# A depthwise 3x3 term moved from VectorE, ScalarE and GpSimd to TensorE, in a fused attention and expert block

## The chip, the core and the metric

The kernel runs on one core of one Trainium2 chip. The metric is the device time of one execution in microseconds (us); lower is better. All data are float32.

## What is computed

The input x is (8, 64, 96, 96). The reference, cut to what matters here:

```python
def _window_attend(xh, qkv_w, lepe_w, bias, sp, heads, scale):      # xh: 32 channels
    qkv = jnp.einsum('oi,bihw->bohw', qkv_w, xh)
    q, k, v = jnp.split(qkv, 3, axis=1)
    lepe = jax.lax.conv_general_dilated(v, lepe_w, (1, 1), 'SAME', feature_group_count=c)
    ...                                                              # windows of 4x4 pixels, 8 heads
    out = jnp.einsum('nhqk,nhkc->nhqc', attn, v) + lepe
    ...
for s in (0, 2):                                                     # plain and rolled by 2
    xs = jnp.roll(x, (-s, -s), axis=(1, 2)) if s > 0 else x          # axes 1, 2: channels, rows
    halves = (xs[:, :c], xs[:, c:])
    ...                                                              # attend each half, roll back
x = x + (results[0] + results[1])                                    # of the normalized x
t = tokens of x
t = t + top-2-of-8 experts (64 to 64 channels each) of the normalized t
```

So there are four attention problems per image (two halves of the channels, plain and rolled by two channels and two rows), each with a depthwise 3x3 convolution of its value channels (`lepe`). Their sum is added to x, and a mixture of eight experts follows.

## The kernel before

**Tiling.** An image has 24 strips of four rows (384 pixels); two strips are a tile, 12 per image and 96 in all. A strip has 24 windows, done in three units of eight windows. The program runs through 576 slots, one per unit, so a strip is 3 slots and a tile is 6 slots. Every step has a lag in slots (`LAG`): in each slot every engine does, in the order in which its body lists them, the steps whose turn it is. Lags set how far apart producer and consumer stand; the engines are otherwise held together by semaphores, and each engine works strictly in its written order. The loop body holds 72 slots (one image) and is written out, so that all instructions of an image are distinct; a head of one image and a tail of nearly two stand outside it.

**Stages.** For each tile the input is loaded, centred and normalized over channels (`centre`, `variance`), and stored to a buffer `xn` in DRAM; from there it is loaded again as strips with all four problems on the 128 partitions (`load_strips`). For each strip TensorE makes the values (`value`, L612), and a second time, in another channel order, the values for the convolution (`wo`, L615); then queries and keys (`query_key`, L624 and L625). GpSimd issues the DMAs that spread keys and values (L516, L528). For each unit TensorE computes the scores (L585, 64 small matmuls with 64 loads), VectorE takes the row maximum and subtracts it (L904, L909), ScalarE exponentiates (L742) and lays the bias for a later unit into the score bank (L748), VectorE transposes (L969), and TensorE forms the products with the values (L652) and, in the last unit of a strip, the sums (L658). ScalarE inverts the sums (L714, L716), VectorE multiplies (`divide`, L922, into `att`).

**The convolution before.** ScalarE copies the values of L615 from PSUM into a padded image `vpad` in SBUF (L737). Of the nine taps ScalarE multiplies three (L780), GpSimd adds these three (L547), and VectorE does the other six as multiply-adds, two per slot (L896). VectorE then adds the result to `att` and reorders it into rows (`add_taps`, L955, into `fin`). SyncE stores `fin` to `z` in DRAM (L427).

**The tile stage.** When all strips that a tile needs are in `z`, SyncE loads x, the plain part `z0t` and the rolled part `z2t` (`load_tile`, ten DMAs, L449 and L454). VectorE adds them (L935, L948), then come a second normalization, the router (L682), the logits turned by TensorE (L636), the choice of two experts on VectorE, the gates turned by three TensorE transposes (L594), stored and spread over partitions by eight DMAs per tile (L474, L484), multiplied into the normalized tokens by VectorE (L884), and four pairs of expert matmuls (L570: two halves of 64 output channels, each with 128 input rows), on top of a bias matmul (L689). VectorE adds and SyncE stores the result.

**What sets the order around the change.** The products of a strip's first unit may only start when `divide` of the strip before has read the one bank of products, `bank_o` (`pe.wait_ge(picked, k)`, L646). The bank `bank_p[1]` is shared by the second value matmul, the keys, the variances and the router; `bank_g` holds the turned gates and the logits. SyncE does its DMA issues and waits in one strict order, and `load_tile` waits there for the `z` it has just stored to land (L438).

## Time and profile before

| | us |
|---|---|
| median of 3 runs | 3483.31 |
| lowest and highest run | 3472.05, 3487.7 |
| the profiled execution: its span, first to last instruction | 3495.3 |
| busy in it: TensorE / VectorE / GpSimd / ScalarE | 3038.4 / 3088.6 / 2932.3 / 2038.3 |
| mean granted TensorE clock, as a share of 2.4 GHz | 0.925 |

The profiled execution's own time was not listed apart from its span; the span lies 0.3% above the median of the runs and 0.2% above the highest. PE is TensorE, DVE VectorE, ACT ScalarE, POOL GpSimd, SP SyncE.
### The profile page before, as it was taken

Reading aid. Unit: us, or ns where it says so; the run is one execution under the profiler, and the core shown is the slowest. Engines: PE = TensorE matmul, PEld = TensorE weight load, DVE = VectorE, ACT = ScalarE, POOL = GpSimd, SP = SyncE. Lnnn points to the kernel's source line nnn. Section 1 sums busy time; section 2 is a strip of 40 time slices with the busy share of each in tenths; the row PEclk is TensorE's granted clock in tenths of the full one; section 3 lists DMA queues with packets and bytes.
Section 4 is the critical chain, followed back from the end, with each engine's and each line's share of the span. In section 5 each row is a group of like instructions: output and inputs, shape, how many; then the busy total and the mean of one; then the engine's idle time right before and its main releaser. Section 6 shows DMA issues by size and latency. Waiting matters only on the chain.

```text
span 3495.3 us, 200950 instructions
## 1 busy us (share of the span) xinstructions
PE 3038.4 (87%) x82372; PEld 1892.0 (54%) x82372; DVE 3088.6 (88%) x6049; ACT 2038.3 (58%) x4130; POOL 2932.3 (84%) x5382
## 2 busy tenths in 40 slices
PE   5889888888898888998888988889899899889886
PEld 3655555555555555555555555555555555555551
DVE  3789999889999888998999889999899899999995
ACT  3666666556565556665666656566556656666651
POOL 5998888888898788987888878889788988888970
PEclk8999999999899899998999989999899989999986
DMA  2345555545555455545555544555455555555555
GB/s 58 85 122 147 137 143 138 143 130 143 136 144 139 125 144 137 145 130 133 136 139 140 139 131 130 143 135 143 130 140 138 143 134 145 137 143 137 138 124 151
DMA packets 427432, 469.79 MB, mean 134 GB/s; under 512 B 117616, under 2 KB 407920, under 8 KB 426480
## 3 DMA queue, kind: packets, MB, share of 16 engines
q1 hardware_dynamic: 260592, 342.97, 36.3%
q0 software_dynamic: 165888, 113.57, 13.5%
q8 instruction: 665, 10.90, 1.4%
q14 instruction: 287, 2.35, 0.2%
HBM read 264.97 MB, written 77.86 MB: 98 GB/s over the span
## 4 chain that ended last, share of the span: by engine, by line
PE 36%; DVE 22%; issue 14%; DMA 12%; SPq 9%; POOL 3%; ACT 3%; DVEq 1%; ACTq 0%; POOLq 0%
PE bank L585 9%; PE bank L652 8%; SPq L454 6%; DMA gate_wide<-gate_rows 6%; DVE lepe L896 6%; DMA z<-fin 5%; PE bank L570 5%; DVE row_max L904 3%; PE bank L658 2%; PE bank L612 2%; POOL vx L528 2%; PE bank L624 2%; DVE probT L969 2%; SPq L449 1%; DVE gx L884 1%
## 5 line engine op out<-in xcount | busy, mean ns | idle before, releaser
L528 POOL DMA_DIRECT2D vx<-vt x3072 | 1555.5, 515 | 201.9 <-PE bank L658 181.0
L652 PEld LDWEIGHTS bank<-probT,vx 128*32 128x32 f32 x36864 | 825.8, 188 | 442.4 <-issue 378.2
L652 PE MATMUL bank<-probT,vx 128*32 128x16 f32 x36864 | 888.2, 234 | 170.7 <-issue 117.5
L516 POOL DMA_DIRECT2D kx<-k_sb x1536 | 738.8, 488 | 230.9 <-issue 114.6
L585 PEld LDWEIGHTS bank<-kx,qx 32*32 32x32 f32 x36864 | 602.9, 112 | 434.9 <-issue 432.2
L585 PE MATMUL bank<-kx,qx 32*32 32x64 f32 x36864 | 709.9, 227 | 128.5 <-issue 90.9
L742 ACT ACTIVATE prob<-prob 128x512 f32<-128x512 f32 x576 | 367.4, 638 | 538.9 <-DVE prob L909 538.6
L896 DVE SCALAR_TENSOR_TENSOR lepe<-vpad,table,lepe 128x384 f32<-128x384 f32 x960 | 630.8, 657 | 0.0
L884 DVE TENSOR_TENSOR gx<-gate_wide,yn_pair 128x768 f32<-128x768 f32 x384 | 393.8, 1026 | 194.4 <-DMA gate_wide<-gate_rows 148.0
L547 POOL TENSOR_TENSOR lepe_p<-lepe_p,tap_sb 128x384 f32<-128x384 f32 x384 | 435.0, 1133 | 39.0 <-issue 18.5
L904 DVE TENSOR_REDUCE row_max<-bank 128x32 f32<-128x512 f32 x576 | 394.4, 685 | 29.5 <-PE bank L585 16.4
L909 DVE TENSOR_TENSOR prob<-bank,row_max 128x512 f32<-128x512 f32 x576 | 398.4, 692 | 16.7
L969 DVE STREAM_TRANSPOSE probT<-prob 128x512 f32<-128x512 f32 x576 | 405.3, 704 | 0.0
L570 PE MATMUL bank<-gx,table 128*64 128x384 f32 x1536 | 357.2, 542 | 15.6 <-DVE gx L884 14.4
L748 ACT ACTIVATE bank<-bias_tile 128x512 f32<-128x512 f32 x576 | 341.0, 592 | 0.0
L538 POOL DMA_DIRECT2D yn_pair<-yn x384 | 201.3, 532 | 67.5 <-DVE gx L884 43.0
L756 ACT ACTIVATE qx<-bank,table 128x384 f32<-128x384 f32 x384 | 200.7, 575 | 62.2 <-PE bank L624 62.1
L780 ACT ACTIVATE tap_sb<-vpad,table 128x384 f32<-128x384 f32 x384 | 232.8, 606 | 2.0 <-POOL lepe_p L547 2.0
L625 PE MATMUL bank<-xs,table 32*32 32x384 f32 x1536 | 200.6, 549 | 14.1 <-issue 14.1
L624 PE MATMUL bank<-xs,table 32*32 32x384 f32 x1536 | 200.1, 545 | 5.2 <-issue 3.8
L735 ACT ACTIVATE v_sb<-bank 128x384 f32<-128x384 f32 x192 | 93.2, 485 | 176.6 <-PE bank L612 173.4
L612 PE MATMUL bank<-xs,table 128*128 128x384 f32 x384 | 169.7, 524 | 20.5 <-DMA xs<-xn 20.5
(75 smaller groups left out, 3801.9 us busy)
## 6 DMA issues: line engine op xcount, KB each, us to landing
gate_wide<-gate_rows SPq DMA_DIRECT2D x768, 192.0 KB
vx<-vt POOLq DMA_DIRECT2D x3072, 12.0 KB
kx<-k_sb POOLq DMA_DIRECT2D x1536, 24.0 KB
z<-fin SPq DMA_DIRECT2D x192, 192.0 KB, 4.3
yn_pair<-yn POOLq DMA_DIRECT2D x384, 96.0 KB
xa<-in_x SPq DMA_DIRECT2D x192, 96.0 KB, 3.3
xn<-xa SPq DMA_DIRECT2D x192, 96.0 KB
xs<-xn SPq DMA_DIRECT2D x96, 192.0 KB
```

The source lines that it names most:

```text
L516: pool.dma_start(kx[to + m:to + C:4, r % 2, m, :], k_sb[at + m:at + C:4, r % 2, :])\
L528: pool.dma_start(vx[to:to + TOK, r % 2, col:col + 13:4, odd, :], vt[at:at + TOK, r % 2, x::2, :, :].rearrange("p h n k -> p h (n k)"))\
L547: G.tensor_tensor(lepe_p[:, kr % 2, :], lepe_p[:, kr % 2, :], tap_sb[:, j - 1, :], ALU.add).then_inc(pool_lepe_made, 1)
L570: last = MM(bank_f[half * C:(half + 1) * C, 0:SPX], const("experts")[:, p * C:(p + 1) * C], gx[:, p % 2, half, :], start=False, stop=(p == ...
L585: last = MM(bank_s[r % 2][at, w * KEYS:(w + 1) * KEYS], qx[at, kr % 2, win, :, :].rearrange("p a i -> p (a i)"), kx[at, kr % 2, :, win * T ...
L652: last = MM(bank_o[32 * c:32 * c + 32, at * TOK:(at + 1) * TOK], vx[:, kr % 2, :, at % 2, at // 2 * 4 + ba], probT[:, kr % 2, at, ba * TOK ...
L742: S.activation(prob[:, r % 4, :], prob[:, r % 4, :], ACT.Exp).then_inc(exp_made, 1)
L884: V.tensor_tensor(gx[:, p % 2, :, :], gate_wide[:, p, :, :], yn_pair[:, r % 2, :, :], ALU.mult)\
L896: V.scalar_tensor_tensor(acc, vrows(r, t // 3 - 1, t % 3 - 1), lepe_taps[:, t:t + 1], first if j == 0 else acc, ALU.mult, ALU.add).then_in ...
L904: V.tensor_reduce(row_max[:, r % 2, :], per_row(bank_s[r % 2][:, :]), AX.X, ALU.max).then_inc(max_made, 1)
L909: V.tensor_tensor(per_row(prob[:, r % 4, :]), per_row(bank_s[r % 2][:, :]), over_keys(row_max[:, r % 2, :]), ALU.subtract).then_inc(shifte ...
L969: V.transpose(probT[:, kr % 2, j * UW:(j + 1) * UW, :].rearrange("p n k -> p (n k)"), prob[:, r % 4, :]).then_inc(probT_made, 1)
```

## The change

The convolution acts on the values, which are a linear map of the normalized x. The change joins both: for each output channel, tap and input channel it builds a weight once at the start (VectorE, from tables: tap times value weight, plain and rolled parts added), so that the four depthwise terms become a single 3x3 convolution from 64 to 64 channels of `xn`, done on TensorE per tile of eight rows, where the sum with x is formed.

- SyncE loads, per tile, ten rows of `xn` twice, the second copy one row further (`load_halo`, two DMAs of 64 partitions by 3840 bytes; four at the two tiles at the image's edge). With two rows on the 128 partitions a matmul does two taps of a column.
- TensorE does three groups of matmuls per tile, one for each column offset, in the slots with lags 34, 35 and 36. A group is four matmuls of 128 rows by 64 columns over 384 pixels: two halves of the tile, which go to the two halves of the PSUM partitions, by two weight sets (rows one and two, row three with zeros). At the edge of an image some are cut into pieces.
- The second value matmul, its copy to `vpad`, and all taps on ScalarE, GpSimd and VectorE are gone; `divide` writes `fin` directly, and PE's wait on `picked` becomes one on `fin_made`, counted on the same instruction. VectorE adds three terms instead of two per tile (`y_first` now reads the convolution's bank).
- The convolution takes `bank_g`. The logits and the gates go through `bank_p[1]`; three transposes of gates become one of 48 columns, and the bias matmul of the experts becomes three over 128 pixels.

The diff, cut to its core:

```diff
 LAG = dict(
     ...
-    tap_products=15, pool_taps=16, taps=19, add_taps=24,
-    store_z=24, load_tile=33, y_first=37, y_second=38, ..., router=41, logits=42,
-    take_logits=43, gates=45, ...
+    store_z=24, load_halo=29, load_tile=33, conv=34, y_first=37, y_second=38, y_third=38, ..., router=41, logits=44,
+    take_logits=44, gates=45, ...
 # SyncE
+                if ti := s.tile("load_halo"):
+                    k, r = ti
+                    if s.later(r, 2):
+                        wait_alone(sp, conv_made, k - 1)
...
+                        put_halo(0, 0, t * (2 * SP) - 1, HALO)
+                        put_halo(1, 0, t * (2 * SP), HALO)
 # GpSimd
-                if st := s.in_strip("pool_taps"):
-                    k, kr, j = st
-                    if j:
-                        pool.wait_ge(tap_made, k * POOL_TAPS + (j + 1))
...
-                        G.tensor_tensor(lepe_p[:, kr % 2, :], lepe_p[:, kr % 2, :], tap_sb[:, j - 1, :],
-                                        ALU.add).then_inc(pool_lepe_made, 1)
 # TensorE
             pe.wait_ge(table_loaded, 16)
+            pe.wait_ge(conv_w_made, 1)
...
-                    for blk in range(TBLK):
-                        last = nc.tensor.transpose(bank_g[0:GE, blk * 128:(blk + 1) * 128],
-                                                   gate_tmp[:, 4, blk * GE:(blk + 1) * GE], const("ident"))
-                    last.then_inc(gateT_made, 1)
+                    nc.tensor.transpose(bank_p[1][0:TBLK * GE, 0:128], gate_tmp[:, 4, :], const("ident"))\
+                        .then_inc(gateT_made, 1)
...
                     MM(bank_p[0][:, 0:SPX], wv, xs[:, r % 4, :], start=True, stop=True).then_inc(v_made, 1)
-                    if r % 2:
-                        pe.wait_ge(ln_made, tiles_to(s, (k - 1) // 2 + 3))
-                    MM(bank_p[1][:, 0:SPX], wo, xs[:, r % 4, :], start=True, stop=True).then_inc(vo_made, 1)
...
+                if (ti := s.in_tile("conv")) and ti[2] < len(SIDES):
+                    k, r, side = ti
+                    t, dw = (r + 1) % IMT, SIDES[side]
+                    if side == 0:
+                        pe.wait_ge(halo_loaded[r % 2], halos_to(s, r) * 16)
+                        if s.later(r, 1):
+                            pe.wait_ge(y_step, k * 2 - 1)
+                    low, high = max(0, -dw), W - max(0, dw)
+                    first = [side == 0, side == 0]
+                    for group, skip in ((0, 0), (1, 2)):
+                        parts = [(half, *rows) for half in range(2) for rows in conv_rows(t, half)[group]]
+                        for half, top, end, which in sorted(parts, key=lambda part: part[1]):
+                            at = half * SP + skip
+                            last = MM(by_rows(bank_c[half * C:(half + 1) * C, 0:SPX])[:, top:end, low:high],
+                                      conv_w[:, which, group * 3 + side, :],
+                                      by_rows(halo[:, r % 2, :])[:, at + top:at + end, low + dw:high + dw],
+                                      start=first[half], stop=(side == 2 and group == 1), skip_group_check=True)
+                            first[half] = False
+                    if side == 2:
+                        last.then_inc(conv_made, 1)
...
-                            pe.wait_ge(picked, k)
+                            pe.wait_ge(fin_made, k)
...
-                    MM(bank_f[:, 0:SPX], const("expert_bias", GE), gateT[:, r % 2, :], start=True, stop=True)
+                    for blk in range(TBLK):
+                        MM(bank_f[:, blk * 128:(blk + 1) * 128], const("expert_bias", TBLK * GE)[:, blk * 128:(blk + 1) * 128],
+                           gateT[:, r % 2, :], start=(blk == 0), stop=True, skip_group_check=True)
 # ScalarE
-                    act.wait_ge(vo_made, k + 1)
-                    S.activation(vrows(r, 0, 0), bank_p[1][:, 0:SPX].rearrange("p (r w) -> p r w", w=W),
-                                 ACT.Copy).then_inc(v_saved, 1)
...
-                    S.activation(product.rearrange("p (r w) -> p r w", w=W), vrows(r, -1, j - 1), ACT.Copy,
-                                 scale=lepe_taps[:, j:j + 1]).then_inc(tap_made, 1)
 # VectorE
-            V.memset(vpad[:, :], 0.0).then_inc(const_made, 1)
             dve.wait_ge(table_loaded, 16)
+            ...                               # seven operations of 128 x 384 or 64 x 384 that build conv_w
...
-                    V.tensor_tensor(att[:, r % 2, :], bank_o[:, 0:SPX], row_inv[:, r % 2, :], ALU.mult).then_inc(picked, 1)
+                    V.tensor_tensor(windows(fin[:, r % 2, :]), by_window(bank_o[:, 0:SPX]),
+                                    by_window(row_inv[:, r % 2, :]), ALU.mult).then_inc(fin_made, 1)
...
-                    V.tensor_tensor(y[:, r % 4, :], xt[:, r % 2, :], z0t[:, r % 2, :], ALU.add).then_inc(y_step, 1)
+                    dve.wait_ge(conv_made, k + 1)
+                    V.tensor_tensor(y[:, r % 4, :], bank_c[:, 0:SPX], xt[:, r % 2, :], ALU.add).then_inc(y_step, 1)
...
-                    V.tensor_tensor(windows(fin[:, r % 2, :]), by_window(att[:, r % 2, :]),
-                                    windows(lepe[:, r % 2, :]), ALU.add).then_inc(fin_made, 1)
...
-                taps = s.in_strip("taps")
-                if taps:
-                    tap(taps[0], taps[1], 2 * taps[2])
...                                           # y_second adds z0t, the new y_third adds z2t
-                if taps:
-                    tap(taps[0], taps[1], 2 * taps[2] + 1)
```

## Rows read from the trace of the kernel before

**Rows 1.** The page: busy us of each engine (share of span) and instructions

```profile
PE 3038.4 (87%) x82372; PEld 1892.0 (54%) x82372; DVE 3088.6 (88%) x6049; ACT 2038.3 (58%) x4130; POOL 2932.3 (84%) x5382
```

**Rows 2.** Busy time by stretch: five of 500 us, the last and their sum

```profile
core 0: us, PE busy (x) PEld busy (x) DVE busy (x) ACT busy (x) POOL busy (x), PEclk, DMA share, GB/s
2500.00:3000.00 500.00, 448.51 (x12219) 280.39 (x12219) 454.17 (x898) 303.41 (x616) 434.28 (x800) 0.94 0.53 138
sum 2500.00, PE 2211.04 PEld 1382.66 DVE 2254.99 ACT 1491.45 POOL 2144.69; mean PE 442.21 PEld 276.53 DVE 451.00 ACT 298.29 POOL 428.94
```

**Rows 3.** Timeline, PE: start us, us; the variance matmul, once per tile, 80 apart

```profile
274.90 0.91 PE L603 MATMUL bank<-sq,table 128*128 128x384 f32 x2
3110.54 0.91 PE L603 MATMUL bank<-sq,table 128*128 128x384 f32 x2
```

**Rows 4.** Chain in order of time, 1757 to 1800: start us, us, what

```profile
1768.48 0.80 PE bank L570 x4
1769.28 0.84 PE bank L612 x2
1770.12 0.65 PE bank L615 x2
1770.77 1.23 issue
...
1774.54 2.54 issue
...
1780.61 1.65 PE bank L672 x2
1782.25 1.86 PE bank L585 x64
...
1785.60 0.66 PE bank L658 x8
...
1787.10 0.84 PE bank L689 x2
1787.94 1.02 PE bank L585 x64
1788.97 0.43 PE bank L594 x3
```

**Rows 5.** Groups of the removed work: busy us, mean ns of one, idle before

```profile
L896 DVE SCALAR_TENSOR_TENSOR lepe<-vpad,table,lepe 128x384 f32<-128x384 f32 x960 | 630.8, 657 | 0.0
L547 POOL TENSOR_TENSOR lepe_p<-lepe_p,tap_sb 128x384 f32<-128x384 f32 x384 | 435.0, 1133 | 39.0 <-issue 18.5 <-POOL lepe_p L547 0.2
```

**Rows 6.** Waits: engine, line, waited for: us in total, times, longest us

```profile
PE bank L652 <- issue: 117.5, 140, 2.0
PE bank L585 <- issue: 90.9, 63, 4.0
PE bank L672 <- ACT k_sb L765: 61.0, 69, 2.1
PE bank L585 <- ACT bank L748: 36.6, 79, 2.3
DVE gx L884 <- DMA gate_wide<-gate_rows: 148.0, 80, 8.5
SPq L337 <- DVE fin L955: 273.3, 159, 14.7
```

**Rows 7.** Timeline, DVE and SP around two PE stalls: start us, us

```profile
1771.35 0.55 DVE L922 TENSOR_TENSOR att<-bank,row_inv 128x384 f32<-128x384 f32 x1
1774.31 2.31 SPq L413 DMA_DIRECT2D xs<-xn  x5
1790.47 2.76 SPq L484 DMA_DIRECT2D gate_wide<-gate_rows  x4
```

**Rows 8.** Busy time in the stretch behind the second stall, columns as in rows 2

```profile
1777.10:1784.00 6.90, 6.74 (x159) 4.20 (x159) 6.62 (x19) 3.47 (x9) 2.74 (x5) 0.50 0.22 70
```

**Rows 9.** One line, L570: duration ns min/median/max, first and last start

```profile
L570 PEld LDWEIGHTS bank<-gx,table x1536: 132/136/232, 235.5 to 3490.3; 128*64 128x64 f32 x192
```

More of the change, by code:

```diff
@@ L79, with conv_rows @@
 EXPERT_AT = {(0, 0): 0, (1, 0): 1, (1, 1): 2, (2, 0): 3}
+SIDES = (0, -1, 1)
+HALO = 2 * SP + 2
+BOTH, ROLLED, PLAIN = 0, 1, 2
+def conv_rows(t, half):
+    rows = [[(0, SP, BOTH)], [(0, SP, BOTH)]]
+    if t == 0 and half == 0:
+        rows = [[(0, 1, ROLLED), (1, 2, BOTH), (2, 3, PLAIN), (3, 4, BOTH)],
+                [(0, 1, BOTH), (1, 2, PLAIN), (2, 4, BOTH)]]
+    if t == IMT - 1 and half == 1:
+        rows[1] = [(0, SP - 1, BOTH), (SP - 1, SP, ROLLED)]
+    return rows
 class Slot:
@@ L213, in lay_tables @@
                 here = (h - 1) % HD if roll and a and b else h
-                one = qkv_w[2 * CH + here * HEADS + m]
-                put("wv", rows, g * CH + h * 8 + y * 4 + b * 2 + a, one)
-                at = (a * 2 + b) * CH + roll * 16 + h * 4 + half * 2 + y
-                put("wo", rows, at, one)
-                put("taps", at, slice(0, 9), lepe_w[here * HEADS + m].reshape(9))
+                put("wv", rows, g * CH + h * 8 + y * 4 + b * 2 + a, qkv_w[2 * CH + here * HEADS + m])
     for g in range(4):
@@ L226, in lay_tables @@
     order = tile_channels()
+    for col, channel in enumerate(order):
+        half, o = channel // CH, channel % CH
+        for roll, name in ((0, "plain"), (ROLL, "rolled")):
+            own = (o - roll) % CH
+            for i in range(CH):
+                for copy in range(2):
+                    put("v_" + name, copy * C + (half * CH + i + roll) % C, col, qkv_w[2 * CH + own, i])
+            taps = lepe_w[own].reshape(3, 3)
+            for side in range(3):
+                dw = SIDES[side] + 1
+                put("taps_" + name, slice(0, C), side * C + col, taps[0, dw])
+                put("taps_" + name, slice(C, 128), side * C + col, taps[1, dw])
+                put("taps_" + name, slice(0, C), (3 + side) * C + col, taps[2, dw])
     for half in range(2):
@@ L266, in metaformer_block @@
         xs = sb("xs", [128, 4, SPX])
[L267 removed]
+        halo = sb("halo", [128, 2, HALO * W])
+        conv_w = sb("conv_w", [128, 3, 6, C])
+        conv_parts = sb("conv_parts", [128, 2, 6, C])
         sq = sb("sq", [128, 2, SPX])
```

140 lines of the change are left out of this document (73 added, 67 removed).

## Prediction

> **What bounds the kernel now.** I read the shares of busy time first. Over the whole program [rows 1] and in steady state [rows 2] TensorE and VectorE are both near 90%, GpSimd at 86%, ScalarE at 60%. No single engine stands out, so the next question is what a tile costs and what part of it each engine works. The same matmul of two tiles 80 apart starts at 274.90 and 3110.54 us [rows 3], so a tile of six slots takes 2835.64 / 80 = 35.45 us. Of that TensorE works 442.21 / 500 = 88.4%, which is 31.35 us, and waits 4.1; VectorE works 451.00 / 500 = 90.2%, 32.0 us, and waits 3.5.
>
> Next, what ends the waits [rows 6]. VectorE's largest is on the gates' DMA, 148.0 us or 1.5 per tile: it is late by SyncE's order, not by TensorE. TensorE waits for ScalarE's key copy (61.0) and for the bias (36.6), and most of the rest is called "issue". Two kinds stand in the chain [rows 4]. The 1.23 us before 1772.00 ends right after VectorE has finished `divide` (1771.35 + 0.55 = 1771.90, [rows 7]): the wait on `picked`, with VectorE late behind its taps. The 2.54 us before 1777.08 lies inside one batch of 64 score matmuls, which waits for nothing between them; it begins as SyncE issues five strip loads [rows 7]. I read it as instructions that come late because their DMA shares the engines with such a burst.
>
> The third cost is the clock. Behind this stall the granted clock is 0.50 (1.2 GHz) for the whole 6.90 us [rows 8], and the score batch takes 1.86 us there against 1.02 at the upper level [rows 4]. The steady stretch shows 0.94 [rows 2], so about 12% of the time is at the lower level, 4.3 us per tile. Most of TensorE's work doubles there, the products (L652) hardly; I estimate a cost of 1.5 us per tile from this (4.3, times 0.9 busy, times three quarters that double, of which half is lost). So TensorE has 31.35 - 1.5 = 29.85 us of work at the upper level, and stalls and clock add 4.1 + 1.5 = 5.6.
>
> **What the change takes from the other engines.** Twelve multiply-adds per tile leave VectorE: the larger group alone is 630.8 us [rows 5], 6.6 per tile, and with the add of the taps about 8 us leave it; one add per tile is new. It would stand near 24 us of 35, and no longer bounds. GpSimd loses 435.0 us [rows 5], ScalarE three tap products and a copy per strip. None of this is a gain in itself: TensorE already works 31.35 us of 35.45, so at most 4.1 us per tile can come from taking work off the others.
>
> **What it adds to TensorE.** The convolution is not in the trace, but its shape is: the expert matmuls L570 are pairs of 128 rows to 64 columns over 384 pixels. A pair takes 0.80 us [rows 4], not twice a full matmul, so the two halves run side by side. A convolution group is two such pairs in a row, so between 2 x 0.80 = 1.60 us and one pair plus one matmul at its following price. That price is 0.65: the second value matmul (same shape as the first) takes 0.65 where the first takes 0.84, and the sums L658, eight instructions in four column groups that follow matmuls of the same shape, take 0.66 altogether [rows 4]. Bounds 1.45 to 1.60; I take 1.47, nearer to L615 and L658, which have the same place behind their own kind. Three groups per tile: 4.4 us, bounds 4.3 to 4.8.
>
> The first matmul of a new shape costs 0.84 - 0.65 = 0.19 us more [rows 4]. The Trainium skill, TensorEngine Tiling (Array Packing), Key Properties, says that a change of the tiling mode drains the array. The trace agrees, and it speaks against this change: the removed matmul L615 never paid it, while each convolution group, alone in its slot, does. Without the drain the sum would be 3 x 0.15 = 0.5 us per tile lower.
>
> **What it takes from TensorE.** Two value matmuls per tile, 2 x 0.65 = 1.3 us. Two of three gate transposes: 0.43 us becomes about 0.2 [rows 4]. The bias matmul of 0.84 us becomes three of a third each: between nothing and three shape overheads (+0.4), and nearest to nothing, since the three are of one shape. Together -1.5 (bounds -1.5 to -1.1).
>
> **Waits.** With 8 us less on VectorE, `divide` follows ScalarE's reciprocal at once, so the `picked` stall goes, and so does most of the wait for the bias, which ScalarE lays only after VectorE has read the bank. I take 1.5 us per tile off: 1.0 of the products' waits and 0.4 for the bias (36.6 / 96) [rows 6], plus a little before the centring matmul, where a convolution group now fills the time. Bounds 0.5 to 2.0. The wait of L672 for the keys (61.0, 0.6 per tile) lies within one slot and stays. New waits on PE: for `halo_loaded`, issued five slots ahead; for `conv_made` on VectorE, one slot behind its producer; for `logit_saved` before the next slot's keys. Queued behind the first are products and centring; five slots, some 30 us, cover it, against 8.5 us for the longest wait on a DMA in [rows 6].
>
> **SyncE and the DMAs.** Two issues more per tile, about 1.2 us at the price of the gates' four (2.76, [rows 7]). SyncE waits 273.3 us for `fin` [rows 6], 2.8 per tile, so they fit, and `fin` comes a slot earlier. But 64 x 3840 bytes twice is 0.49 MB, right behind the gates' four loads in that slot. A burst of that kind is what the 2.54 us stall stood behind. Its price per tile lies between nothing (it falls where no instructions are due) and 2.5; I take 0.3, since such stalls occur in some tiles only: 63 gaps before L585 in 96 tiles, 90.9 us [rows 6].
>
> **Clock.** Fewer stalls and denser matmuls leave the upper level longer: -0.4 per tile, bounds -1.5 (never low) and +0.5 (more array work at the lower level).
>
> **The sum.** Per tile: +4.4 - 1.5 - 1.5 + 0.3 - 0.4 = +1.3 us, so 36.75. Some 90 of 96 tiles run at the full rate: +117 us. At the start TensorE waits for a larger table and for seven small VectorE operations, while the 8 us clearing of `vpad` goes: +5. The profiled execution would take 3495.3 + 122 = 3617; it is 0.34% above the median of the runs, so the forecast is 3617 x 3483.31 / 3495.3 = 3605 us, with 3520 to 3690 as its own range from the bounds above.
>
> **The rivals.**
> *TensorE's stalls were VectorE's lag, and go with it: faster.* Its work would be 29.85 + 4.4 - 1.5 = 32.75 us at the upper level; it is faster as soon as stalls and clock fall below 35.45 - 32.75 = 2.7 us per tile, from 5.6. At 1.7 the tile takes 34.45: 90 us less, 3399. For it: VectorE's gap closes, and a dense TensorE keeps its clock. Against: gaps inside L585 and the wait of L672 have nothing to do with VectorE. Chance 0.20.
>
> *The rows loaded twice hold up instructions:* a 2.5 us stall with about 1.5 us of lower clock behind it, in every second tile: +2.0 per tile on the forecast, 180 us, 3784. For it: exactly that stands behind the strip loads [rows 4, 7]. Against: a DMA of rows of 3840 bytes is short. Chance 0.15.
>
> *Halves that do not run side by side* (the change then does not do what it says): twelve matmuls of 0.65 and three overheads, 8.3 us instead of 4.4: +350, about 3950. L570 speaks against it. Chance 0.04.
>
> *Weight loads that lie bare.* A group's loads all use all 128 rows; were none hidden, twelve loads per column half of 0.136 us [rows 9] would add 1.6 us per tile: +146, 3750. The Trainium skill, TensorE: Matmul & The Clock Gate, Part 3, says that weight loads overlap running matmuls only where their row groups differ. The pair's 0.80 us speaks against it, since two loads and two passes of each half leave no room. Chance 0.04.
>
> *No change:* the additions meet the waits, 1.3 us less per tile: 3466 to 3501. Chance 0.10.
>
> **How the numbers follow.** Forecast 0.47, rivals as above. Anything within 0.5% is about what a measurement of this kernel cannot tell from no change. Faster 0.20, same 0.10, slower 0.70. The range takes in the upper half of the faster case (from 3400) and the lower half of the burst case (to 3765); half of each and the 0.04 of serial halves are left out, about 0.2.
>
> **What would show it.** Each group of four convolution matmuls takes 1.45 to 1.6 us at the upper level and halves start together. VectorE falls to two thirds of the span, GpSimd to three quarters, TensorE rises above 90%. The wait before the products' first matmul vanishes; gaps inside batches stay near 1.5 us per tile. The granted clock rises slightly above 0.93. The prediction is wrong if a group takes more than 2 us, if TensorE's idle time falls below 1 us per tile, or if gaps inside batches double.

## Result and profile after

The changed kernel takes 3502.88 us (median of 7 runs, 3497.51 to 3515.66), the kernel before 3487.7 on the same chips: a ratio of 1.0059, 95% interval 1.0038 to 1.008. It is slower by 0.6%, where 3.5% were forecast. The profiled execution spans 3499.1 us.

The engines' busy time (the page, columns as in [rows 1]), then the last of the five steady stretches and their sum (columns as in [rows 2]; the five clocks are 0.97, 0.97, 0.97, 0.96, 0.99), then the variance matmul of two tiles 80 apart (timeline, answering [rows 3]):

```profile
PE 3221.6 (92%) x84772; PEld 1980.6 (57%) x84772; DVE 2232.8 (64%) x4807; ACT 1618.5 (46%) x3362; POOL 2501.4 (71%) x4998
...
2500.00:3000.00 500.00, 472.90 (x12717) 292.97 (x12716) 334.73 (x731) 241.64 (x504) 373.82 (x749) 0.99 0.58 154
sum 2500.00, PE 2339.46 PEld 1441.21 DVE 1625.79 ACT 1180.74 POOL 1822.34; mean PE 467.89 PEld 288.24 DVE 325.16 ACT 236.15 POOL 364.47
...
277.58 0.91 PE L638 MATMUL bank<-sq,table 128*128 128x384 f32 x2
3117.42 0.91 PE L638 MATMUL bank<-sq,table 128*128 128x384 f32 x2
```

A tile takes 2839.84 / 80 = 35.50 us, against 35.45 before. VectorE fell from 32.0 to 23.1 us of it, TensorE rose from 31.35 to 33.2 and waits 2.3 instead of 4.1. The mean granted clock of the five stretches is 0.97, so the lower level takes some 5.6% of the time, 2.0 us per tile. Before, the five show 0.94, 0.94, 0.93, 0.92 and 0.94, which is 4.7 us per tile (the prediction took the last alone, 4.3).

The convolution's own pieces, and its neighbours, in the chain (start us, us, what), and TensorE's waits, answering [rows 4, 6]. L687 is the convolution, L647 the value matmul, L630 the transpose, L746 the bias matmul, L707 the products, L622 the scores, L727 the matmul after the keys:

```profile
1721.50 0.86 PE bank L746 x6
1723.38 0.22 PE bank L630
1724.26 1.43 PE bank L687 x8
1730.41 1.43 PE bank L687 x8
...
PE bank L707 <- issue: 91.6, 91, 2.9
PE bank L622 <- issue: 54.6, 36, 4.1
PE bank L727 <- ACT k_sb L819: 32.9, 48, 1.4
PE bank L622 <- ACT bank L802: 7.9, 14, 2.3
```

A group of the convolution takes 1.43 us at the upper level, three of them 4.3 per tile. All four waits of TensorE are shorter than before [rows 6]: that before the products went from 117.5 to 91.6 us, that before the scores from 90.9 to 54.6, that of the scores for the bias from 36.6 to 7.9, that of L727 for the keys (L672 before) from 61.0 to 32.9. The profile calls "issue" both a wait before the first matmul of a batch and a gap inside the batch. Taken apart by place in the trace, all waits before a batch of products fell from 103.5 to 9.4 us, as was forecast; the gaps inside batches went from 65.3 to 87.1 us for the products and from 75.5 to 37.4 for the scores, together from 140.8 to 124.5.

What VectorE and SyncE wait for now (us in total, times, longest), which the runs below need:

```profile
DVE fin L966 <- ACT row_inv L773: 358.1, 93, 6.3
DVE gx L939 <- DMA gate_wide<-gate_rows: 270.8, 94, 8.0
SPq L358 <- DMA z<-fin: 496.1, 95, 6.7
SPq L358 <- DMA gate_rows<-gateT: 235.5, 92, 4.8
```

VectorE has room and waits for ScalarE and for the gates (270.8 us for 148.0 before); SyncE waits for its own stores, and its wait for `fin` fell from 273.3 to 21.8 us, so it has little slack left.

### The profile page after: what moved, and what is told of

It reads as the page before. It is cut to its first block, busy times and chain, and to the rows that moved or that the text cites. A ratio compares the mean times of both kernels' runs of the same rounds, so it can differ in the third digit from the quotient of the medians.

```text
span 3499.1 us, 202400 instructions
## 1 busy us (share of the span) xinstructions
PE 3221.6 (92%) x84772; PEld 1980.6 (57%) x84772; DVE 2232.8 (64%) x4807; ACT 1618.5 (46%) x3362; POOL 2501.4 (71%) x4998
## 4 chain that ended last, share of the span: by engine, by line
PE 81%; issue 6%; DVE 5%; ACT 4%; DMA 2%; SPq 2%; DVEq 0%; ACTq 0%
PE bank L707 19%; PE bank L622 16%; PE bank L687 12%; PE bank L607 9%; PE bank L713 4%; PE bank L647 3%; PE bank L660 3%; PE bank L727 3%; PE bank L638 2%; PE bank L721 2%; PE bank L732 2%; PE bank L746 2%; PE bank L738 2%; ACT qx L810 1%; ACT bank L802 1%
## 5 line engine op out<-in xcount | busy, mean ns | idle before, releaser
L707 PEld LDWEIGHTS bank<-probT,vx 128*32 128x32 f32 x36864 | 830.1, 190 | 396.2 <-issue 372.3
L707 PE MATMUL bank<-probT,vx 128*32 128x16 f32 x36864 | 891.8, 234 | 104.8 <-issue 91.6
L622 PEld LDWEIGHTS bank<-kx,qx 32*32 32x32 f32 x36864 | 570.1, 108 | 317.4 <-issue 302.6
L622 PE MATMUL bank<-kx,qx 32*32 32x64 f32 x36864 | 672.1, 221 | 63.1 <-issue 54.6
L939 DVE TENSOR_TENSOR gx<-gate_wide,yn_pair 128x768 f32<-128x768 f32 x384 | 365.9, 954 | 479.5 <-DMA gate_wide<-gate_rows 270.8
L796 ACT ACTIVATE prob<-prob 128x512 f32<-128x512 f32 x576 | 364.7, 633 | 245.1 <-DVE prob L951 228.2
L687 PE MATMUL bank<-halo,conv_w 128*64 128x380 f32 (+6 forms) x2592 | 449.8, 472 | 0.1
L946 DVE TENSOR_REDUCE row_max<-bank 128x32 f32<-128x512 f32 x576 | 382.7, 664 | 37.1 <-PE bank L622 31.9
L607 PE MATMUL bank<-gx,table 128*64 128x384 f32 x1536 | 345.4, 528 | 16.1 <-DVE gx L939 13.1
L966 DVE TENSOR_TENSOR fin<-bank,row_inv 128x384 f32<-128x384 f32 x192 | 106.2, 553 | 373.3 <-ACT row_inv L773 358.1
L687 PEld LDWEIGHTS bank<-halo,conv_w 128*64 128x64 f32 x2592 | 169.3, 140 | 231.6 <-issue 218.7
L836 ACT ACTIVATE yrstd<-bank,table 128x384 f32<-128x384 f32 x96 | 55.7, 580 | 356.4 <-PE bank L732 356.4
L647 PE MATMUL bank<-xs,table 128*128 128x384 f32 x384 | 171.0, 527 | 20.7 <-DMA xs<-xn 20.7
L660 PE MATMUL bank<-xs,table 32*32 32x384 f32 x1536 | 179.7, 509 | 7.8 <-issue 6.5
```

Source lines behind the costliest of these rows:

```text
L607: last = MM(bank_f[half * C:(half + 1) * C, 0:SPX], const("experts")[:, p * C:(p + 1) * C], gx[:, p % 2, half, :], start=False, stop=(p == ...
L622: last = MM(bank_s[r % 2][at, w * KEYS:(w + 1) * KEYS], qx[at, kr % 2, win, :, :].rearrange("p a i -> p (a i)"), kx[at, kr % 2, :, win * T ...
L687: last = MM(by_rows(bank_c[half * C:(half + 1) * C, 0:SPX])[:, top:end, low:high], conv_w[:, which, group * 3 + side, :], by_rows(halo[:, ...
L707: last = MM(bank_o[32 * c:32 * c + 32, at * TOK:(at + 1) * TOK], vx[:, kr % 2, :, at % 2, at // 2 * 4 + ba], probT[:, kr % 2, at, ba * TOK ...
L796: S.activation(prob[:, r % 4, :], prob[:, r % 4, :], ACT.Exp).then_inc(exp_made, 1)
L939: V.tensor_tensor(gx[:, p % 2, :, :], gate_wide[:, p, :, :], yn_pair[:, r % 2, :, :], ALU.mult)\
```

## Experiments

All ratios are to the kernel before on the same chip, and a ratio is turned into us by the median of 3487.7. Line numbers are those of each run's own kernel. The chain is the work that ended last, followed back from the end of the execution. Names that begin with b are edits of the kernel before, with a of the changed kernel. "Later" means `load_tile=34` for 33.

| run | edit | ratio | 95% interval |
|---|---|---|---|
| b_no_wo | second value matmul left out | 0.9954 | 0.9933 to 0.9974 |
| b_one_tap | one of six taps on VectorE | 0.9581 | 0.955 to 0.9612 |
| b_no_pool | no adds on GpSimd | 0.9802 | 0.9769 to 0.9835 |
| a_dead_taps | dead taps back on VectorE | 1.0484 | 1.045 to 1.0518 |
| a_no_conv | neither loads nor matmuls of the convolution | 0.9382 | 0.9355 to 0.9408 |
| a_no_mm | its loads alone | 0.9848 | 0.9826 to 0.9871 |
| a_no_halo | its matmuls alone | 0.9923 | 0.9896 to 0.995 |
| a_split | strip loads in two portions | 1.0099 | 1.0068 to 1.0131 |
| a_no_mm_act | loads alone, issued by ScalarE | 1.0057 | 1.0032 to 1.0081 |
| a_halo_act | changed kernel, loads issued by ScalarE | 1.0171 | 1.0141 to 1.0202 |
| a_tile_later | changed kernel, later | 0.9925 | 0.99 to 0.995 |
| a_both | the last two edits | 1.0009 | 0.9991 to 1.0027 |
| b_tile_later | kernel before, later | 0.9763 | 0.9733 to 0.9793 |
| a_no_conv_later | a_no_conv, later | 0.9292 | 0.9263 to 0.932 |
| a_no_mm_later | a_no_mm, later | 0.9618 | 0.958 to 0.9656 |
| a_half_later | half of the matmuls, later | 0.975 | 0.9721 to 0.9779 |
| b_no_wo_later | b_no_wo, later | 0.9817 | 0.979 to 0.9845 |
| b_one_tap_later | b_one_tap, later | 0.9486 | 0.9461 to 0.9511 |

### What set the time before: one part taken away at a time

**b_no_wo: work off TensorE alone.**

```diff
-                    MM(bank_p[1][:, 0:SPX], wo, xs[:, r % 4, :], start=True, stop=True).then_inc(vo_made, 1)
...
-                    S.activation(vrows(r, 0, 0), bank_p[1][:, 0:SPX].rearrange(...
+                    S.activation(vrows(r, 0, 0), bank_p[0][:, 0:SPX].rearrange(...
```

> The kernel before without the second value matmul (L615) on TensorE alone; ScalarE's copy into the padded image stays and takes the first value matmul's bank instead, so the taps work on values in another channel order. Theory 'TensorE's path set the time before': 2 x 0.65 us per tile leave that path, 125 us less (ratio 0.964), or some 60 us less if part of it turns into a longer wait for VectorE's divide. Rival 'VectorE's queue set the time before': no change, within 0.5%.

Measured 0.9954: 16 us, not 125, and within the 0.5% of the rival. TensorE's share, its wait before the products, and VectorE's share in this run:

```profile
PE 2934.9 (85%) x81988; PEld 1834.0 (53%) x81988; DVE 3089.7 (89%) x6049; ACT 2024.0 (58%) x4130; POOL 2943.5 (85%) x5382
PE bank L651 <- issue: 200.6, 186, 2.4
PE bank L651 <- DVE att L920: 49.9, 46, 2.4
```

TensorE's busy time fell by 104 us, and its waits at the products grew from 117.5 [rows 6] to 200.6, and those on `divide` from 24.8 to 49.9; all waits before a batch of products from 103.5 to 181.7. The mean granted clock fell from 0.925 to 0.914. VectorE is as busy as it was. TensorE's work alone did not set the time before: most of what it was spared turned into waiting before the products.

**b_one_tap: work off VectorE alone.**

```diff
                 if taps:
-                    tap(taps[0], taps[1], 2 * taps[2])
+                    if taps[2] == 0:
+                        tap(taps[0], taps[1], 0)
...
                 if taps:
-                    tap(taps[0], taps[1], 2 * taps[2] + 1)
+                    pass
```

> The kernel before with one of VectorE's six multiply-adds per strip instead of six; five taps are left out of the sum, everything else stays. It measures what VectorE's lag costs by itself: 10 x 0.657 us per tile leave VectorE and nothing leaves TensorE. By the prediction's terms for waits and clock (1.5 + 0.4 per tile) 180 us less (ratio 0.948); by what the trace of the change shows for them (1.85 + 0.9) 260 us less (ratio 0.925). If VectorE never mattered: no change.

Measured 0.9581, 146 us, less than either account had expected (180 and 260). The multiply-adds that are gone had taken 630.8 us [rows 5]; VectorE's busy time fell by 542 us, and about a quarter of that arrives: soon something else is late. The engines, the chain (shares of the span by engine), and the longest waits of VectorE and SyncE:

```profile
PE 2989.2 (89%) x82372; PEld 1873.9 (56%) x82372; DVE 2546.8 (76%) x5089; ACT 2057.2 (61%) x4130; POOL 2905.7 (87%) x5382
PE 33%; SPq 19%; DMA 18%; issue 13%; DVE 8%; POOL 5%; ACT 2%; DVEq 0%; ACTq 0%; POOLq 0%
DVE gx L884 <- DMA gate_wide<-gate_rows: 346.3, 101, 7.9
SPq L337 <- DMA z<-fin: 482.0, 95, 6.6
```

SyncE's queue and the DMAs hold 37% of it, and VectorE's wait for the gates grew from 148.0 to 346.3 us: SyncE's order and its transfers come next.

**b_no_pool: work off GpSimd alone.**

```diff
-                        G.tensor_tensor(lepe_p[:, kr % 2, :], lepe_p[:, kr % 2, :], tap_sb[:, j - 1, :],
-                                        ALU.add).then_inc(pool_lepe_made, 1)
...
-                        dve.wait_ge(pool_lepe_made, (k + 1) * (POOL_TAPS - 1))
+                        dve.wait_ge(tap_made, k * POOL_TAPS + 1)
```

> The kernel before without GpSimd's two adds per strip (two of the nine taps are left out of the sum); VectorE and TensorE keep all their instructions. Theory 'TensorE's path and VectorE's lag': GpSimd has slack, so at most 0.5% faster. Rival 'GpSimd's adds hold up VectorE's instructions that run beside them': VectorE gains up to 1 us per tile, and the time falls by 1 to 3%.

ScalarE's wait for these adds goes with them. Measured 0.9802, 69 us: the rival. The engines, two groups of VectorE's instructions (busy us, mean ns), and the second of them in the kernel before:

```profile
PE 3033.5 (88%) x82372; PEld 1899.0 (55%) x82372; DVE 2831.9 (83%) x6049; ACT 2049.8 (60%) x4130; POOL 2501.1 (73%) x4998
L890 DVE SCALAR_TENSOR_TENSOR lepe<-vpad,table,lepe 128x384 f32<-128x384 f32 x960 | 568.9, 593 | 0.0
L836 DVE TENSOR_TENSOR gate_tmp<-gate_tmp,table 128x48 f32<-128x48 f32 x192 | 36.2, 189 | 3.4
...
L842 DVE TENSOR_TENSOR gate_tmp<-gate_tmp,table 128x48 f32<-128x48 f32 x192 | 75.3, 392 | 3.4
```

VectorE does the same 6049 instructions in 2831.9 us instead of 3088.6. The multiply-adds take 593 ns for 657 [rows 5]. The multiply of 48 columns has the same median, 207 ns, in both runs, but its longest takes 1914 ns with the adds and 215 without: few instructions are hit, and these for long. So GpSimd's 435.0 us of adds cost VectorE 257. GpSimd's own DMA issues can go out sooner too; how much of the 69 us that gives, no run separates. The Trainium skill, SBUF — State Buffer, Who interferes with whom, says that a VectorE instruction with two SBUF inputs contends with a GpSimd instruction that reads SBUF; these have two such inputs, and the run agrees.

**a_dead_taps: VectorE's load back on the changed kernel.**

```diff
+                dead = s.unit("turn_p")
+                if dead:
+                    dead_tap(dead)          # scalar_tensor_tensor, 128 x 384, result unused
...
+                if dead:
+                    dead_tap(dead, 1)
```

> The changed kernel with two dead multiply-adds per slot put back on VectorE (128 x 384 each, results unused), so that VectorE carries the old load of taps beside the new convolution. Theory 'VectorE's lag costs TensorE stalls and clock': the stalls before the products come back, 180 to 260 us more (ratio to before 1.06 to 1.08). Rival 'on the changed kernel TensorE is so long that VectorE has room for both': no change against the changed kernel (ratio 1.006).

Measured 1.0484, 0.0425 above the changed kernel, about 148 us: below the 180 to 260 that were expected, and far from no change. The engines, and TensorE's wait for the keys:

```profile
PE 3339.4 (91%) x84772; PEld 2035.0 (55%) x84772; DVE 2797.8 (76%) x5961; ACT 1635.0 (44%) x3362; POOL 2510.1 (68%) x4998
PE bank L730 <- ACT k_sb L822: 87.0, 86, 2.3
```

TensorE does the same 84772 instructions, but is busy 118 us longer, with the mean granted clock at 0.926 instead of 0.963 (0.926 to 0.939 in the four runs, 0.959 to 0.963 in the seven of the changed kernel); and its wait for the keys is 87.0 us instead of 32.9. The stalls before the products, which were to come back, did not: 6.0 us before a batch for 9.4; the gaps inside batches are 128.2 for 124.5. VectorE is only 76% busy here, and still it costs TensorE that much, in clock and in the wait for the keys.

### The price of the convolution's two parts

```diff
 # a_no_mm: the twelve matmuls out, the count kept
-                        last.then_inc(conv_made, 1)
+                        pe.sem_inc(conv_made, 1)
 # a_no_halo: rows loaded for the first two tiles only; a_no_conv: both edits
-                if ti := s.tile("load_halo"):
+                if (ti := s.tile("load_halo")) and s.turn is None and ti[0] < 2:
```

> The changed kernel without the convolution: no matmuls of it and no loads of its rows after the first two tiles, so the term is missing and only the removal of the old taps and the moved gate steps are left. By the prediction's own terms (1.5 removed, 1.5 waits, 0.4 clock per tile) 306 us less than before (ratio 0.912). Theory 'VectorE and GpSimd set the time before, and TensorE with its own stalls sets it once they are lighter': TensorE is left with 28.4 us of work per tile, and with 3 to 4 us of stalls and clock the ratio is 0.88 to 0.92. If VectorE with GpSimd had been only part of the story: above 0.94, no better than what five taps less gave (0.958).

> The changed kernel with the row loads of the convolution but without its matmuls (the term is missing). Against the run with neither, it prices the loads by themselves where TensorE has some room: forecast 0.3 us per tile, 27 us; rival 'the loads hold up instructions': 100 to 180 us.

> The changed kernel with all convolution matmuls, which read rows loaded once for the first two tiles (the term is wrong from the third tile on). Against the changed kernel it prices the loads where TensorE is full: 27 us by the forecast, nothing if the measured trace is read rightly (its gaps inside batches did not grow), 100 to 180 us by the rival. Against the run with neither it prices the matmuls: 4.3 us per tile, 390 us, if all of it lies on the path that sets the time; less if TensorE had room.

The runs without the rows also leave out TensorE's wait for them. Without either part 0.9382: taking the old convolution away is worth 216 us, not the 306 of the sum; no account had this value. The loads alone add 0.0466 (163 us, the rival's size), the matmuls alone 0.0541 (189 us, not 390). Beside each other they cost less: the loads 0.0136 (47 us) once the matmuls are there, the matmuls 0.0211 (74 us) once the loads are there. Two things that each fill a time of their own, side by side, behave so. What the matmuls do is seen in a_no_conv and a_no_halo, which differ in them alone. The pages of both, and the convolution's group in a_no_halo:

```profile
PE 2870.3 (88%) x82182; PEld 1836.9 (56%) x82182; DVE 2221.7 (68%) x4807; ACT 1635.4 (50%) x3362; POOL 2509.1 (77%) x4998
...
PE 3199.1 (93%) x84772; PEld 1969.9 (57%) x84772; DVE 2234.8 (65%) x4807; ACT 1620.1 (47%) x3362; POOL 2510.1 (73%) x4998
L688 PE MATMUL bank<-halo,conv_w 128*64 128x380 f32 (+6 forms) x2592 | 446.0, 471 | 2.1 <-issue 2.1
```

The matmuls are busy 446 us, but TensorE's busy time grows by 329 only, and its idle time (the spans 3271.1 and 3451.3 less the busy time) falls from 400.8 to 252.2 us. The mean granted clock is 0.932 without them and 0.964 with them. So they fill time in which TensorE waited, and all its other instructions together take 117 us less at the higher clock. The largest part of the idle time that goes is gaps inside the batches of scores and products, 144.5 to 78.9 us; why these shrink beside the convolution stays open. VectorE is equally light in both runs. It is much the same with the tile loads later, where SyncE counts for less: a_no_conv_later leaves TensorE idle for 368.8 us at 0.934, a_tile_later, with both parts, for 266.1 at 0.967.

The chains, by engine, of a_no_conv, a_no_mm and a_no_halo, in this order:

```profile
PE 45%; SPq 17%; DMA 17%; issue 11%; DVE 6%; ACT 3%; DVEq 0%; ACTq 0%
...
SPq 34%; DMA 29%; PE 22%; issue 11%; DVE 2%; ACT 2%; DVEq 0%; PEld 0%; ACTq 0%; PEldq 0%
...
PE 78%; DVE 8%; issue 6%; ACT 5%; DMA 1%; SPq 1%; DVEq 0%; ACTq 0%
```

With the loads alone SyncE's queue and its DMAs are 63% of the chain, with the matmuls alone TensorE is 78%. The prediction had looked for the loads' price in late instructions. TensorE's "issue" waits at the scores in a_no_conv and a_no_mm, then at the scores and the products in a_no_halo, bear on that:

```profile
PE bank L623 <- issue: 85.6, 62, 3.9
PE bank L623 <- issue: 156.4, 110, 3.5
...
PE bank L622 <- issue: 42.3, 19, 3.7
PE bank L708 <- issue: 55.8, 78, 2.0
```

The changed kernel has 54.6 and 91.6 in place of the last two. The gaps inside batches alone grow by 46 us (78.9 to 124.5) where the rows are loaded beside the matmuls, as much as the loads cost there, and by 69 us of 163 (144.5 to 213.3) without the matmuls. So part of the price has the place that the prediction gave it; that it is instructions that come late there is not shown. The rest, without the matmuls, stands in SyncE's queue and in the transfers that SyncE and VectorE wait for.

**a_split: are the gaps inside TensorE's batches made by the burst of strip loads?**

```diff
+                if ti := s.tile("load_plain"):          # lag 6; the plain half of load_strips, lag 9
+                    ...
-                    put(slice(0, C), 0, slice(0, C), t * (2 * SP), 2 * SP)
```

> The changed kernel with the strip loads in two portions: the plain half (192 KB) three slots earlier, the rolled half where it was. Theory 'instructions of TensorE come late because their DMA stands behind a burst of loads': the gaps inside batches after the strip loads halve, 20 to 60 us less with the clock that they cost (ratio to before 0.99 to 1.0). Rival 'the gaps have another cause': no change against the changed kernel (1.006).

Measured 1.0099, no faster than the changed kernel. The waits called "issue":

```profile
PE bank L715 <- issue: 84.6, 95, 2.3
PE bank L630 <- issue: 57.7, 42, 3.9
```

They are what they were (91.6 and 54.6). Moving half of the burst away does not change these gaps; their cause stays open.

### SyncE's order

**The loads on another queue.**

```diff
-                        sp.dma_start(halo[copy * C:(copy + 1) * C, r % 2, at * W:(at + n) * W],
+                        act.dma_start(halo[copy * C:(copy + 1) * C, r % 2, at * W:(at + n) * W],
```

> The run with the row loads and without the convolution's matmuls (the term is missing), with these loads issued by ScalarE instead of SyncE: the same bytes at about the same place, but out of SyncE's order. Theory 'SyncE's order sets the time there; the loads cost their issues (1.5 us per tile) in it': the cost of the loads goes, ratio 0.938 to 0.95 as without them. Rival 'the bytes cost: DMA engines and late instructions': it stays near 0.985.

> The changed kernel with the convolution's row loads issued by ScalarE. Theory 'SyncE's order': the 1.4% that the loads cost beside full TensorE goes in good part, ratio 0.992 to 0.998. Rival 'the bytes': 1.006 as the changed kernel. Should ScalarE's issues hold up its copies: above 1.006.

ScalarE also takes over the wait for `conv_made` and gets waits for the stores of `xn`. Both got slower, 1.0057 for 0.9848 and 1.0171 for 1.0059. Neither theory says that of a_no_mm_act; of a_halo_act it was to mean that the issues hold up ScalarE's copies. They do a little: TensorE's wait for the keys is 50.3 us in a_no_mm_act and 23.4 in a_no_mm, but ScalarE is 2% of the chain. The longest waits of VectorE and SyncE in a_no_mm_act, and SyncE's for the same store in a_no_mm:

```profile
DVE gx L933 <- DMA gate_wide<-gate_rows: 590.2, 96, 13.4
SPq L358 <- DMA gate_rows<-gateT: 426.2, 93, 7.3
...
SPq L358 <- DMA gate_rows<-gateT: 279.1, 91, 5.5
```

SyncE loses the issues, but waits 426.2 us for the gates' store to land, where it had waited 279.1 with the loads in its own order, and VectorE waits 590.2 us for the gates instead of 443.9. Without the rows (a_no_conv) SyncE waits 187.5 us for it. From the end of that store's issue to the next spread of gates it takes, in the median tile, 3.9 us without the rows, 4.8 with the rows issued by SyncE and 6.6 with the rows issued by ScalarE. So the rows do make this short store land later, and more so from ScalarE's queue. Why more so is argued, not shown: issued by SyncE, the rows come where SyncE has got to; issued by ScalarE, they come on time, beside the store.

**The tile loads one slot later.**

```diff
-    store_z=24, load_halo=29, load_tile=33, ...
+    store_z=24, load_halo=29, load_tile=34, ...
```

> The changed kernel with SyncE's tile loads one slot later (lag 34 for 33), so that it no longer stands waiting for the z that it has just stored (4.9 us per tile in the traces). Theory 'SyncE's order': that wait goes and gives SyncE slack, ratio 0.99 to 1.0. If SyncE has no part in the changed kernel's time: 1.006. If the loads then come too late for VectorE: above.

> Both: row loads issued by ScalarE and tile loads one slot later. With SyncE out of the way TensorE's order alone should be left: the ratio of the run with the matmuls and without the loads, 0.992, or down to 0.98 if SyncE's lateness was part of that too. By the rival 'the bytes': 1.0 to 1.006.

a_tile_later 0.9925: faster than both kernels, and at the ratio of the matmuls without loads (0.9923). a_both 1.0009, between the two edits: not the 0.98 to 0.992 of the theory, but what the rival 'the bytes' had for it. The waits of SyncE and VectorE in a_tile_later:

```profile
SPq L358 <- DMA z<-fin: 454.3, 95, 6.9
DVE gx L939 <- DMA gate_wide<-gate_rows: 14.7, 6, 5.0
```

The theory's size was right and its place was not: SyncE's wait for z stays at 454.3 us (496.1 in the changed kernel). What went is VectorE's wait for the gates, 270.8 us, which is 14.7 in this run. In slot 33 the third pair of gate loads had stood behind ten tile loads in SyncE's order; one slot later it goes first. That this wait is what cost the 1.3% is not shown: a_no_halo has the same ratio with 218.8 us of it, and a_both has 54.0 us of it at 1.0009.

**The same on the kernel before, and on the parts.**

> The kernel before with SyncE's tile loads one slot later (lag 34 for 33), nothing else; the third pair of gate loads then goes out ahead of them. Theory 'VectorE with GpSimd's adds sets the time before, SyncE only adds the wait for the gates to it (148 us in the trace)': that wait goes, and 40 to 140 us with it, ratio 0.96 to 0.99. Rival 'SyncE set the time before as it does without the convolution': below 0.96. If VectorE merely waits elsewhere: 1.0.

> The changed kernel without convolution matmuls and without its row loads after the first two tiles (the term is missing), with the tile loads one slot later. Theory 'there SyncE's order sets the time (0.938), not TensorE': it falls clearly, to 0.90 to 0.92. Rival 'TensorE with its stalls sets it': no change, 0.935 to 0.94.

> The changed kernel with the row loads but without the convolution's matmuls (the term is missing), with the tile loads one slot later. Theory 'the row loads cost in SyncE's order': their price of 165 us shrinks to 30 to 90 us over the run without them, ratio 0.92 to 0.95. Rival 'their bytes cost whatever the order': it stays 165 us above that run.

> The changed kernel with the tile loads one slot later and without the second weight set of the convolution (the third row of taps is missing): two of four matmuls of a group, 0.64 us at the upper level, three times per tile. Theory 'TensorE's order sets the time of the changed kernel': 1.93 us per tile, 185 us, less than with them (0.9925 to 0.94). Rival 'by then SyncE or VectorE sets it': half of that or less (above 0.965).

b_tile_later 0.9763, 83 us for one number in `LAG`; it is the fastest complete version. VectorE's waits for the gates and its share:

```profile
DVE gx L884 <- DMA gate_wide<-gate_rows: 15.4, 7, 6.5
PE 3028.0 (89%) x82372; PEld 1897.0 (56%) x82372; DVE 3144.9 (92%) x6049; ACT 2045.9 (60%) x4130; POOL 2931.0 (86%) x5382
```

The wait of 148.0 us [rows 6] is nearly gone, and VectorE is now 92% busy. The chain is 43% TensorE and 31% VectorE; b_no_wo_later tells which of them counts. a_no_conv_later 0.9292 is only 0.009 better than a_no_conv, between the theory (0.90 to 0.92) and the rival: there TensorE's order (70% of the chain) is close behind SyncE's. a_no_mm_later 0.9618: the loads still cost 0.0326, 114 us for 163, where the theory had 30 to 90. The order explains a third of their price; of what is left, 57 us are gaps inside TensorE's batches (146.7 to 203.7), the other half stays open. a_half_later 0.975: half of the matmuls saves 0.0175, 61 us of 185, as the rival had it. Even with TensorE at 92% and 79% of the chain, a third of its work counts. The rest goes back into waits and clock: TensorE is idle for 301.6 us instead of 266.1, and the mean granted clock is 0.935 instead of 0.967.

> The kernel before without the second value matmul on TensorE (ScalarE's copy takes the first one's bank, so the taps work on values in another channel order) and with the tile loads one slot later. Beside the run with the later loads alone (0.9763). Theory 'VectorE's queue sets the time of the kernel before once SyncE is out of the way': the 1.3 us per tile of TensorE still give next to nothing, 0.970 to 0.977. Rival 'it was SyncE's order that hid them': 1.3 us per tile, ratio 0.94 to 0.955.

> The kernel before with one of six multiply-adds per strip on VectorE (five taps are left out of the sum) and the tile loads one slot later. Without the later loads the five taps gave 0.958, and SyncE's order stood in that run's chain. Theory 'VectorE's queue, then SyncE's order': both gains add, 0.92 to 0.935. Rival 'TensorE's own work stops it near there': 0.945 to 0.955.

b_no_wo_later 0.9817 (beside 0.9763 for the later loads alone): TensorE's 1.3 us give nothing where SyncE has slack, so it was not SyncE's order that hid them; VectorE's is left. The ratio is even above the 0.970 to 0.977 of the theory, and no run tells why. b_one_tap_later 0.9486, in the range of the rival: with most taps gone the later loads bring 0.0095 instead of 0.0237; the gains do not add, and TensorE's order (72% of the chain) is what is left.

## Why the prediction was wrong

**The bound.** "No single engine stands out" was read rightly, but the sum then took TensorE's order as the base and counted in full what leaves it and what comes to it. The runs show VectorE's order, with the gates that SyncE brings late, as what set the time before: 1.3 us per tile off TensorE gave 0.17 (b_no_wo), and nothing with SyncE relieved; 6.6 us off VectorE gave 1.5; one slot in SyncE's order gave 0.9 (b_tile_later); GpSimd's adds, which the prediction called no gain, gave 0.7, and VectorE's instructions are shorter without them. All that leaves the other engines and TensorE was to give 3.4 us per tile (1.5, 1.5 and 0.4); a_no_conv measured 2.25.

**The sum, term by term, in TensorE's account.** Convolution: 4.3 us per tile measured for 4.4. Removed from TensorE: 1.3, and the transposes 0.43 to 0.22; the bias matmul 0.86 for 0.84: right. The mis-sized terms are waits and clock. Waits: 4.1 to 2.3 us, so -1.8, where the sum had -1.5 and +0.3 for the loads. The waits before the products gave the 1.0 (103.5 to 9.4 us), and the bias 0.3 of its 0.4. The wait for the keys, which was to stay, gave 0.3. The gaps inside batches stay near 1.5 (1.5 to 1.3), but two terms cancel in them: the rows add 0.5 (a_no_halo to the changed kernel) for 0.3, and the convolution's matmuls take 0.7 away (a_no_conv to a_no_halo), which the sum did not have. Clock: the lower level fell from 4.7 to 2.0 us per tile, by the prediction's own factor 1.6 to 0.7, so -0.9 for -0.4. Together 4.3 - 1.5 - 1.8 - 0.9 = +0.1, against +1.3 forecast and +0.05 measured.

**The step that failed** is the overlap of the convolution with TensorE's own waits. The prediction put its 4.4 us on top in full, let the waits shrink almost only by what leaves VectorE, and took 0.4 for the clock. The runs show that the matmuls pay for more than half of themselves: they are busy 446 us, 4.6 per tile at the clock of that run, and cost 189 us, 2.0 per tile (a_no_halo beside a_no_conv), because TensorE's idle time falls from 400.8 to 252.2 us and its mean clock rises from 0.932 to 0.964. VectorE's relief alone does not give that: a_no_conv has it in full, with the idle time at 400.8 us for 456.9 before, and a clock of 0.926 to 0.932 in its runs where the kernel before has 0.926 to 0.934 on the same chip (with SyncE's order relieved 368.8 us, and 0.934 in the profiled execution). It is needed all the same. With dead taps back on VectorE the profiled execution is 179 us longer; 118 of them are TensorE's busy time, at a clock of 0.926 for 0.963, and 54 the wait for the keys.

That wait, of which the prediction said that it "lies within one slot and stays", fell to 20.5 us in b_one_tap and to 32.9 in the changed kernel, from 61.0, and went to 87.0 with the dead taps. ScalarE, which copies the keys, may stand between: in its order the exponential, which waits for VectorE's subtraction, comes ahead of that copy, and ScalarE's own wait for the subtraction was 538.6, 236.0, 228.2 and 401.7 us in the kernel before, b_one_tap, the changed kernel and a_dead_taps. But a_no_halo, with VectorE light, waits 57.6 us for the keys, so this is not the whole of it. The gaps inside the batches of scores have little to do with VectorE, as the prediction said: dead taps leave them at 39.5 us for 37.4.

**The sign** was right, but hung on one number. Against the kernel before as it stood, the changed kernel with its tile loads one slot later is faster (0.9925). With the loads later in both, the change makes the kernel 1.7% slower (0.9925 beside 0.9763), half of what was forecast.

**The rivals.** "TensorE's stalls were VectorE's lag" was right that waits and clock shrink further, and its threshold held, 2.7 us per tile of stalls and clock; 2.3 + 0.7 = 3.0 were left, so the result stopped just short of it. It had the cause in part only, since the convolution itself takes most of them. It deserved more than 0.20, and the forecast less. "The rows loaded twice hold up instructions" named a cost that exists, 47 us in the changed kernel, where gaps inside batches grow by as much, and 163 without the matmuls; it had put it at 180, in stalls of 2.5 us with low clock behind them. What it never weighed is SyncE's order as a limit: SyncE's slack of 2.8 us before `fin` was counted as free, though ten loads further on SyncE is late for the gates. Halves side by side and hidden weight loads: 1.43 us per group rules both rivals out. No change (3466 to 3501) was 2 us short of the median.

## What to carry to other kernels

With several queues at 85 to 90% there is no base to which prices may be added: price each queue by taking a known piece off it alone, and expect under half of it to arrive. Work added to an engine that waits costs less than its own time as well: here 446 us of matmuls cost 189, and 74 beside the loads. A queue that only issues transfers belongs to them, though no page counts it as busy: look for a consumer waiting on a DMA whose issue stands behind others (here 148 us of VectorE), and try moving a step by one place before rebuilding a stage. TensorE's clock belongs to the sum: here it rose when matmuls filled its waits (0.932 to 0.964) and fell when VectorE was loaded again (0.963 to 0.926).

## What was new about the hardware

- GpSimd's adds lengthen VectorE's instructions beside them: 6049 instructions take 3088.6 us with 435.0 us of adds and 2831.9 without; the 48-column multiply takes 392 ns on average with them and 189 without, its longest 1914 and 215.
- The same 84772 TensorE instructions take 3221.6 us at a mean clock of 0.963 and 3339.4 at 0.926; only VectorE's load differs.
- Twelve matmuls more per tile raise the mean granted clock from 0.932 to 0.964, and TensorE's other instructions take 117 us less for it.
- Loads moved to another engine's queue made one of SyncE's own short stores land later (279.1 to 426.2 us of waiting), and the kernel slower by 2% without the convolution's matmuls and by 1% with them.
